# Two mask instructions of VectorE move ahead of the normalization of the probabilities in step 0

## What is computed

```python
x = x + xattn(layernorm(x), ctx)     # 8 heads of 64 over 257 context rows of width 192
x = x + attn(layernorm(x))           # gated linear recurrence over the 32 rows, 4 heads
x = x + ffn(layernorm(x))            # low-rank: gelu(x U1 V1 + b1) U2 V2 + b2
```

## Time and profile before

| what | value |
|---|---|
| median of three runs | 1034.33 us (1033.14 to 1035.65) |
| the profiled execution's own time | 1032.74 us |
| its span, first to last instruction | 1030.9 us |
| busy in the span: PE, DVE, ACT, POOL | 93%, 60%, 59%, 36% |
| mean granted clock of TensorE | 0.975 |

### The profile page before, as it was taken

How to read it: one execution, slowest core, us unless ns; L and a number is a source line. 1 busy time by engine, 2 the same in 40 slices (tenths; PEclk the granted TensorE clock), 3 DMA queues, 4 the chain that set the end, 5 groups by cost and what they waited for, 6 DMA issues and landing times.

```text
span 1030.9 us, 23431 instructions
## 1 busy us (share of the span) xinstructions
PE 959.1 (93%) x8968; PEld 788.0 (76%) x8968; DVE 614.3 (60%) x1285; ACT 607.1 (59%) x1487; POOL 373.5 (36%) x484
## 2 busy tenths in 40 slices
PE   4889999999999999999999999999999999999987
PEld 3668788786868878787887868778686887867775
DVE  3664857483765737467583755748375674836452
ACT  3555667476565756657475665747566574764532
POOL 1323535152352514335251433515234351523230
PEclk9899999999999999999999999999999999999999
DMA  8323222122212222222212213221221322222000
GB/s 284 102 67 112 75 93 74 58 73 76 93 57 86 71 68 84 75 78 73 85 48 92 83 49 104 74 70 61 82 87 57 101 64 65 68 66 73 3 11 21
DMA packets 58013, 79.03 MB, mean 77 GB/s; under 512 B 10288, under 2 KB 39856, under 8 KB 57904
## 3 DMA queue, kind: packets, MB, share of 16 engines
q1 hardware_dynamic: 56192, 76.38, 24.0%
q10 hardware_dynamic: 1712, 1.16, 0.4%
HBM read 73.05 MB, written 4.46 MB: 75 GB/s over the span
## 4 chain that ended last, share of the span: by engine, by line
PE 76%; DVE 9%; ACT 7%; issue 6%; POOL 1%; DMA 0%; DVEq 0%; POOLq 0%; ACTq 0%
PE gb L356 15%; PE gb L479 8%; PE scores L415 7%; PE acc L446 6%; PE acc L442 6%; PE scores L419 5%; PE ptp L429 5%; PE acc L447 4%; PE gb L598 3%; DVE xn L819 3%; PE gb L588 3%; ACT probs L664 2%; PE gb L388 2%; DVE probs L832 2%; PE gb L540 2%
## 5 line engine op out<-in xcount | busy, mean ns | idle before, releaser
L1060 POOL TENSOR_TENSOR t_l<-raw_t,t_h 128x516 fp32r<-128x516 f32 x128 | 167.6, 1310 | 245.1 <-PE scores L419 180.5
L664 ACT ACTIVATE probs<-scores,small 128x257 f32<-128x257 f32 x256 | 119.1, 471 | 138.2 <-DVE small L825 138.0
L825 DVE TENSOR_REDUCE small<-scores 128x2 f32<-128x514 f32 x128 | 88.3, 690 | 130.9 <-PE scores L419 130.6
L1069 POOL TENSOR_TENSOR ptm<-probs,head 128x32 f32<-128x32 f32 x128 | 35.2, 275 | 266.9 <-DVE probs L832 266.9
L832 DVE TENSOR_TENSOR probs<-probs,small 128x514 f32<-128x514 f32 x128 | 101.7, 795 | 4.4
L479 PE MATMUL gb<-pc,wv 128*64 128x256 f32 (+1 forms) x512 | 64.5, 466 | 30.4 <-issue 30.2
L429 PE MATMUL ptp<-ident,probs 128*128 128x128 f32 x512 | 79.2, 278 | 13.7 <-DVE probs L832 12.3
L446 PE MATMUL acc<-pt,raw_n 128*128 128x256 f32 x256 | 89.9, 433 | 0.0
L415 PE MATMUL scores<-t_h,qk_h 128*128 128x258 f32 x256 | 84.0, 328 | 2.2 <-DVE qk_l L877 2.2
L442 PE MATMUL acc<-pt,raw_n 128*64 128x128 f32 x1024 | 83.5, 284 | 2.2 <-ACT pt L675 0.4
L675 ACT ACTIVATE pt<-ptp 128x512 f32<-128x512 f32 x128 | 77.2, 603 | 13.4 <-PE ptp L429 11.8
(11 more groups left out here) (172 smaller groups left out, 2861.7 us busy)
## 6 DMA issues: line engine op xcount, KB each, us to landing
raw_t<-in_ctx_t SPq DMA_DIRECT2D x128, 258.0 KB, 3.1
raw_n<-in_ctx_n SPq DMA_DIRECT2D x128, 192.0 KB, 2.4
xb<-in_x SPq DMA_DIRECT2D x16, 256.0 KB, 4.3
vsp<-tail_values SPq DMA_DIRECT2D x256, 2.0 KB
out<-ob SPq DMA_DIRECT2D x16, 256.0 KB, 2.8
xin<-in_x SPq DMA_DIRECT2D x15, 256.0 KB, 3.0
khat<-in_wq ACTq DMA_DIRECT2D x1, 512.0 KB, 4.3
wv<-in_wv SPq DMA_DIRECT2D x1, 512.0 KB, 6.2
```

What stands on the lines that cost most here:

```text
L664: go(probs[n % 2][:, r, 0:L], scores[:, r, 0:L], ACT.Exp, bias=nmax[:, r:r + 1], accum_out=rsum[:, r:r + 1]).then_inc(s["exp_ready"], 1)
L825: v_.tensor_reduce(nmax[:], scores[:, :, 0:L], AX.X, ALU.max, negate=True)\
L1060: p_.tensor_tensor(t_l[m % 2][:], raw_t[m % RING][:], t_h[m % 2][:].bitcast(F32), ALU.subtract)\
```

## The change

The two entries for S2 and S3 move in VectorE's table from gap 2 of step 0 to gap 1 of step 0, which is between the row maxima of batch n+1 and the normalization of its probabilities. Nothing else differs: no instruction is added, removed or changed, and the other engines' programs are the same.

```diff
-            GAPS = [[["psp-1"], [], ["S2-2", "S3-2", "WV0-1", "WV1-1"]],
+            GAPS = [[["psp-1"], ["S2-2", "S3-2"], ["WV0-1", "WV1-1"]],
                     [[], [], ["O2-2", "Y3-3", "Y1-1"]],
```

## The result

The changed kernel takes 983.52 us (median of four runs, 981.56 to 984.72), against 1034.95 us for the kernel before beside it (1033.14 to 1035.65): a ratio of 0.9504, 95% interval 0.9482 to 0.9526. The forecast was 985.7 us in a range from 982 to 992, so the result is 2.2 us from it. The profiled execution took 984.72 us with a span of 982.9 us; the forecast on that footing was 984.9.

The account below looks back on a forecast made before the run. The prediction took TensorE, busy 93% of the span, as the bound. From the profiled 1032.74 us it took 30.2 (stall) + 17.6 (clock) = 47.8 us, giving 984.9; between that and 986.5 it chose 985.7 us, range 982 to 992.

Parts of the forecast that it names:

- The masks' new place: VectorE, between row maxima and normalization: the mask pair takes 0.8 us in 2.68 us of idle time, at no cost.
- The stall, 30.2 us: TensorE ahead of WV: the bank of S2 is drained earlier, removing 2.32 us in step (9, 0), 30.2 us in 13 steps.
- The clock, 17.6 us: TensorE in WV: 11 clock falls of 1.6 us each go with the stall, 17.6 us.
- rival 2: In WV, the stall goes but the clock falls stay, belonging to the small matmuls' pattern: 1002.5 us, chance 0.09.
- Slack behind WV, 4.4 us: Transpose of batch n+1 behind WV: of 8.3 us slack for its probabilities, 4.4 are left, so the gain comes through.
- rival 1: Part comes back, through late ScalarE or VectorE work or clock falls elsewhere: 2.6 to 13 us, 988 to 999 us, chance 0.10.
- Elsewhere: Outside i = 3 to 15: order or idle-time cover unchanged, 12.3 us ahead of the transposes and the kernel's end stay.
- the sum: Whole kernel: 30.2 + 17.6 = 47.8 us off the profiled execution's 1032.74 us, giving 984.9 us.
- the two footings in the forecast: Whole kernel: 984.9 us from the profiled execution, or 986.5 us if the median's 1.6 us excess is kept; 985.7 taken.

Follow-up runs that it names:

- another bank: Kernel before with WV done ahead of Qf in step 0, masks left in place, so Qf takes the bank of S2 instead of WV: 989.66 us, ratio 0.9565.
- the short wait: Changed kernel with WV at i = 3 to 15 also waiting for the exponentials of batch n+1: 999.17 us, ratio 0.9652.

## Why the prediction was right, point by point

1. *The masks' new place: no cost.* Right. The pair took 0.78 us against 0.8, and the reciprocal stayed 3.38 us behind the maxima's start. The kernel with one mask shows besides that half of the move would do.
2. *The stall, 30.2 us.* Right in cause, and a little small in size. The cause was argued from the code and two other rounds, because the profile named no releaser; the kernels with one mask and with another bank show it, and in the latter the profile names L924 itself. The size: in rounds at full clock on both sides the prediction had 59.6 - 2.3 = 57.3 us, and 57.0 were measured. The term left out some 0.2 to 0.3 us for each stop, 3 to 4 us in all. The view "idle" counts from the modelled end of the last matmul to the start of the next one; matmuls that follow each other without a stop overlap there (WV starts 1.78 us after Qf, whose matmuls are listed with 1.95 us), and that overlap is lost as well. From Qf's start to WV's start the gain is 4.27 - 1.78 = 2.49 us, not 2.32. Another 0.1 us of a round has no name.
3. *The clock, 17.6 us.* Right, as the five matmuls in the idle time show: 1.6 us for each of the ten falls between WV at i = 3 and i = 15, which is what the prediction had. The medians, 1016.46 against 1035.48 us, are 19 us apart and not 17.6, which goes with the granted clock of the executions of the kernel before that stand beside this run (0.970 to 0.974, against 0.975 in the profiled execution that the prediction was made from). Choosing the rounds at i = 2 and 16 as the nearest rows was what decided it, and rival 2 with its 0.09 falls with this run. By the strict reading of the Trainium skill ("TensorE: Matmul & The Clock Gate", section "HAM oscillation — how this bites in real kernels") a wait as short as this should have left the clock alone; the runs disagree, with falls in 11 of 13 rounds at 2.3 us and in 9 of 13 at 2.0 us, and decide.
4. *Slack behind WV, 4.4 us.* Nearly right: the probabilities are ready at 528.24 and the transposes start at 532.35, 4.1 us later. No other wait took the place of this one, so the first half of rival 1, something late on another engine, did not come. Its second half, falls of the clock in other places, is the next point.
5. *Elsewhere.* Not quite still. Up to WV at i = 3 the changed kernel gained only 184.31 - 184.18 = 0.13 us where the stop alone was worth 2.5, and from WV at i = 15 to the end it took 982.9 - 868.23 = 114.67 us against 1030.9 - 915.37 = 115.53, 0.9 less where the fall in WV alone was worth 1.6.

Of the kernel before, one wait of TensorE and two stretches (with the granted clock as the third number from the end) that stand against this:

```profile
PE gb L365 <- DVE xn L819: 10.7, 4, 8.4
...
60.00:66.00 6.00, 5.87 (x60) 4.20 (x60) 3.75 (x8) 4.42 (x11) 2.35 (x4) 1.00 0.11 33
996.00:1004.00 8.00, 5.49 (x93) 3.69 (x94) 3.90 (x6) 3.90 (x10) 3.10 (x3) 1.00 0.01 2
```

And of the changed kernel the same two places:

```profile
60.00:66.00 6.00, 5.80 (x44) 4.07 (x45) 3.63 (x8) 4.17 (x11) 3.01 (x4) 0.72 0.00 0
948.00:956.00 8.00, 7.03 (x93) 4.53 (x94) 3.13 (x5) 4.00 (x10) 2.32 (x2) 0.79 0.01 2
```

The first normalization came later (TensorE waited 8.9 us for it, not 8.4), and the clock fell once near 60 us and once near 950 us where it had not in the kernel before. (Both traces have another fall, some 92 us before their end.) The change does not touch these places. The kernel with one mask, which starts WV just as early, has neither fall in its trace (the same stretch near 60 us, and the one at the same distance from the end):

```profile
60.00:66.00 6.00, 5.87 (x58) 4.33 (x57) 4.02 (x8) 4.86 (x13) 2.71 (x3) 1.00 0.11 27
945.60:953.60 8.00, 5.49 (x93) 3.70 (x94) 3.89 (x6) 3.90 (x10) 3.09 (x3) 1.00 0.01 2
```

Its span is 980.5 us, 50.4 less than that of the kernel before. Of the nine traces of this case three have the fall near 60 us (the changed kernel, the one with five matmuls and the one that waits for the probabilities) and two the fall near the end (the changed kernel and the one with another bank). So these falls are not tied to the change; what decides them was not looked into. Two falls of 1.6 us are why 3 us more than predicted in the steady rounds ended as 48.0 us in the span, against the 47.8 of the sum.

So the closeness on the span is in part small errors that cancel: stops that cost more than their idle time, and falls elsewhere. On the profiled execution's footing the miss is 0.2 us. The other 2 us of the 2.2 are the step from there to the median: the forecast added 0.8 us, and the median lies 1.2 us below the profiled execution. The granted clock goes the same way: the four executions took 984.72, 984.33, 982.70 and 981.56 us at 0.990, 0.990, 0.991 and 0.993. The choice between the two footings in the forecast was a guess at how many falls the other executions have.

## What to carry to other kernels

When a dealt-out buffer makes the bottleneck engine wait, look for the instruction that frees it and for what that instruction is queued behind; here one copy of 0.4 us stood behind a wait that it had nothing to do with, and moving it ahead was worth 5%, over a third of it by the clock. An idle time of TensorE can cost more than its length: ask the granted clock of the stretch behind it, and compare with a round that has no such stop. A wait whose releaser the profile doesn't name can be settled from the trace alone by places in the same program where the buffer happens to be another one.

## What the runs showed of the hardware

- Idle time of TensorE of 2.0 and 2.3 us ahead of a run of matmuls was followed by the clock's lower level in 9 and 11 of 13 cases, 1.1 us in none; a fall cost 1.6 us. Extra matmuls that nobody needs, in place of the idle time, made a kernel 19 us (1.8%) faster.
- A stop costs TensorE 0.2 to 0.3 us beyond the idle time that the profile shows (58.34 - 57.0 - 1.1 with the short wait; 59.6 - 57.0 - 2.3 in the kernel before).
- A matmul of 128x128 by 256 fp32 columns takes 0.43 us back to back and stands as two records of 0.21 us spacing in the trace: ten of them were 20 records in 4.58 us at i = 3, the first of them behind Qf. Whoever takes the spacing of the records for the price of a matmul gets half.
